# A cross-attention and low-rank FFN kernel: written-out engine orders for the first three batches, up and down weights in eight pieces, and a value chunk ahead of the row transposes

## The chip, the cores and the metric

The kernel runs on one core of a Trainium2 chip. The metric is the device time of one execution in microseconds, from that core. The kernel before took 1092.97 us in the median of three runs (1090.92 to 1093.71). Engines: PE is TensorE, ACT is ScalarE, DVE is VectorE, POOL is GpSimd, SP is SyncE, which only issues DMAs here. `PEld` is TensorE's weight load.

## The reference

Thirty-two independent batches, each a 128 x 1024 matrix in float32 (channels by time), pass through a windowed cross-attention and a routed low-rank FFN:

```python
x = x + xattn(layernorm(x), ctx, Wq, bq, Wk, bk, Wv, bv, Wo, bo)
x = x + ffn(layernorm(x), gate_w, lora_A, lora_B)

# xattn: q = Wq x + bq, k = Wk ctx + bk, v = Wv ctx + bv (128 x 128 weights)
k_win, v_win = k[:, :, idx], v[:, :, idx]       # window of 16 keys per query, zero padded
dots = einsum('bhdt,bhdtw->bhtw', q, k_win) * scale     # 8 heads of 16
out  = einsum('bhtw,bhdtw->bhdt', softmax(dots), v_win)
return Wo out + bo

# ffn: rows of 1024, 8 experts of rank 64, top 2 of them
w_full = top-2 of softmax(x @ gate_w.T), normalised
out = sum_e w_full[:, e] * (x @ lora_A[e].T @ lora_B[e].T)
```

The layer norms run along the 1024 columns.

## The kernel before

**Tiles.** A batch is one tile of 128 partitions by 1024 columns. Every matmul operand of the projections and of the FFN is split into two float32r parts, hi and lo (`x_split`, `ctx_split`, `attn_split`, `mid_split`, `ht_split`, and for the weights `w_split`, `down_split`, `up_split`), and a product is three passes (hi hi, hi lo, lo hi). ScalarE writes the hi part (a copy that rounds), and VectorE or GpSimd the lo part (exact minus hi). The weights are split once, at the start, in pieces: each lands in a buffer that is not needed yet, is split from there, and the buffer is then free for its own use. Before, there are six pieces: `w_split` (512 columns), two of `up_split` (2048 each) and three of `down_split` (2048, 1024, 1088).

**Attention.** The queries are laid out as small diagonal blocks (`q_diag`), two batches deep. The scores of a batch come in four chunks of 512 columns on PSUM banks `bank_b0` and `bank_b1` in turn, each opened with the mask in it: `scores_chunk(b, m)`, 64 small float32 matmuls, 128 in the trace. VectorE takes the maximum and subtracts it (`scores_shift`), ScalarE does the exponentials in `prob`, VectorE sums and inverts (`weights_sum`), GpSimd scales (`weights_norm`), VectorE transposes into `prob_t` (`weights_transpose`). The value chunks, `weighted_chunk(b, m)`, go to `bank_b2` and `bank_b3`; ScalarE (`even_heads`) and VectorE (`join_heads`) bring each into `attn`. The values themselves are transposed by VectorE (`v_transpose`) and scattered by four DMAs into the block-diagonal `v_diag` (`place_v`).

**FFN.** The second norm's result `xn2` is transposed on PE (eight 128 x 128 blocks into `bank_a`, `L371`), split, multiplied by the down weights (`down(0, f)` holds the router's logits too), routed on VectorE (`choose_experts`, `gate_experts`; ScalarE's `gap_exponential` in between), weighed (`h_sb`), transposed, split and multiplied by the up weights (`up`). `add_mixture` adds to the residual, and SP stores it.

**Order of the work.** Each engine has a list written out by hand, and semaphores alone join the lists. A step works on five batches at once: in step n, `cur` is batch n (values, scores and the first two value chunks), `ahead` is n+1 (queries, keys, first scores), `later` is n+2 (loads and first norm), `prev` is n-1 (last value chunks, output projection, second norm) and `old` is n-2 (FFN). Steps -2 to 33 are the same code with parts left out where a batch does not exist. PE is unrolled fully; the other engines loop over steps 3 to 28, two per turn. Each engine runs its list strictly in order, so an instruction that waits holds all behind it. `bank_c` is shared by the four projections, which therefore wait for each other's evacuation: `place_q` (`L575`), `evacuate_k` (`L583`), `evacuate_v` (`L591`), `residual` (`L848`). In many places PE's wait for a chunk is written one matmul product early, so that it stands ahead of the last product before the chunk:

```python
for n in range(6):
    if n == 5 and cur:
        open_scores(cur, 3)
    last = project_pass(n, bank_c, 1, ctx_split)
```

## Time and profile before

| what | value |
|---|---|
| median of three runs | 1092.97 us |
| the profiled execution | 1090.87 us |
| its span in the trace | 1089.1 us |
| PE busy | 1003.8 us, 92% |
| VectorE busy | 842.4 us, 77% |
| ScalarE busy | 573.7 us, 53% |
| GpSimd busy | 429.5 us, 39% |
| mean granted clock of TensorE | 0.978 |

Busy time is that of instructions, without waits. The granted clock is a share of 2.4 GHz, and 0.5 is the lower level, 1.2 GHz. A row of the timeline gives the start, the time from the first start to the last end, engine, line, operation, tiles, shapes and count; in brackets stands the idle time of the engine just ahead of it, and what ended that ("issue" where the trace shows no releaser). float32 matmuls are two passes each in the trace, so a score chunk counts x128 and a value chunk x36.

### The profile page before, as it was taken

How to read it: one execution, taken by the hardware profiler on the slowest of the kernel's cores; microseconds unless marked ns; L12 is line 12 of the kernel's file. 1: busy time of each engine (PE TensorE's matmuls, PEld its weight loads, DVE VectorE, ACT ScalarE, POOL GpSimd, SP SyncE). 2: the span in 40 equal slices, each digit the busy share in tenths (PEclk: the TensorE clock that was granted, in tenths of full speed). 3: DMA queues.
4: the chain of work that ended last, by engine and by line, in shares of the span. 5: the costliest groups of instructions: out<-in, count | busy, mean ns of one | idle time of the engine just before them, and what ended most of it. 6: DMA issues, size and time to landing. Idle time of an engine off the chain costs nothing.

```text
span 1089.1 us, 54694 instructions
## 1 busy us (share of the span) xinstructions
PE 1003.8 (92%) x24452; PEld 867.9 (80%) x24452; DVE 842.4 (77%) x1890; ACT 573.7 (53%) x809; POOL 429.5 (39%) x370
## 2 busy tenths in 40 slices
PE   4657999999999999999999999999999999999977
PEld 2545888888888888888888888888888888888865
DVE  2545798888888888888878878887877888887853
ACT  4544565556655555565555546555555655555321
POOL 3375344344343443443434334343434434342210
PEclk9867999999999999999999999999999999999989
DMA  5321233333321333333223333322333332232210
GB/s 195 101 80 36 84 83 82 100 100 101 100 76 67 79 84 97 100 100 87 66 88 81 81 100 100 95 60 83 81 83 100 100 83 69 89 81 63 61 40 39
DMA packets 157289, 92.47 MB, mean 85 GB/s; under 512 B 139680, under 2 KB 139808, under 8 KB 156704
## 3 DMA queue, kind: packets, MB, share of 16 engines
q1 hardware_dynamic: 157088, 89.25, 28.7%
q8 instruction: 192, 3.15, 1.2%
q14 instruction: 9, 0.07, 0.0%
HBM read 55.16 MB, written 16.78 MB: 66 GB/s over the span
## 4 chain that ended last, share of the span: by engine, by line
PE 88%; issue 3%; POOL 3%; ACT 2%; DVE 2%; SPq 1%; DMA 1%; DVEq 0%
PE bank_a L312 35%; PE bank_b L362 18%; PE bank_c L312 17%; PE bank_b L341 14%; PE bank_a L371 4%; POOL x_split L974 1%; POOL down_split L940 1%; SPq L248 0%; POOL up_split L940 0%; DMA ident<-ident_in 0%; DMA v_diag<-v_t 0%; ACT up_split L542 0%; ACT raw L622 0%; ACT x_split L622 0%; DVE stats L715 0%
## 5 line engine op out<-in xcount | busy, mean ns | idle before, releaser
L362 PEld LDWEIGHTS bank_b<-prob_t,v_diag 64*64 64x64 f32 x4608 | 193.4, 136 | 48.0 <-issue 33.1
L362 PE MATMUL bank_b<-prob_t,v_diag 64*64 64x96 f32 (+2 forms) x4608 | 208.8, 242 | 20.7 <-DVE attn L732 9.0
L312 PE MATMUL bank_a<-down_split,mid_split 128*128 128x264 f32 (+1 forms) x1536 | 214.9, 289 | 1.1 <-issue 0.5
L947 POOL TENSOR_TENSOR prob<-prob,row_inv 128x512 f32<-128x512 f32 x128 | 134.6, 1052 | 186.7 <-DVE row_inv L802 185.6
L312 PEld LDWEIGHTS bank_a<-down_split,mid_split 128*128 128x128 f32 x1536 | 194.8, 189 | 8.2 <-issue 1.6
L341 PEld LDWEIGHTS bank_b<-k_sb,q_diag 32*32 32x32 f32 x16384 | 155.5, 105 | 57.2 <-issue 51.4
L341 PE MATMUL bank_b<-k_sb,q_diag 32*32 32x32 f32 x16384 | 172.3, 195 | 25.2 <-issue 22.7
L312 PE MATMUL bank_a<-up_split,ht_split 128*128 128x512 f32 x768 | 192.2, 400 | 3.0 <-DVE ht_split L837 3.0
L312 PEld LDWEIGHTS bank_a<-up_split,ht_split 128*128 128x128 f32 x768 | 139.4, 188 | 32.9 <-ACT ht_split L637 3.4
L953 POOL TENSOR_TENSOR ctx_split<-raw,ctx_split 128x1024 fp32r<-128x1024 f32 x31 | 73.3, 2366 | 183.9 <-ACT ctx_split L603 183.9
L809 DVE STREAM_TRANSPOSE prob_t<-prob 128x768 f32<-128x768 f32 x128 | 124.1, 969 | 23.8 <-POOL prob L947 23.7
L798 DVE TENSOR_REDUCE row_sum<-prob 128x16 f32<-128x512 f32 x128 | 85.3, 667 | 52.0 <-ACT prob L562 52.0
L575 ACT ACTIVATE q_diag<-bank_c,bq_scaled,consts 128x1024 f32<-128x1024 f32 x64 | 73.6, 1200 | 67.3 <-PE bank_c L312 67.3
L784 DVE TENSOR_REDUCE row_max<-bank_b 128x16 f32<-128x512 f32 x128 | 86.3, 674 | 26.6 <-PE bank_b L341 26.3
L312 PE MATMUL bank_c<-ctx_split,w_split 128*128 128x512 f32 x384 | 105.6, 412 | 0.7 <-DVE w_split L705 0.7
L583 ACT ACTIVATE k_sb<-bank_c,bias 128x1024 f32<-128x1024 f32 x32 | 35.6, 1114 | 130.3 <-PE bank_c L312 130.3
L968 POOL TENSOR_TENSOR attn_split<-attn,attn_split 128x1024 fp32r<-128x1024 f32 x32 | 75.6, 2362 | 69.4 <-ACT attn_split L610 69.4
L974 POOL TENSOR_TENSOR x_split<-raw,x_split 128x1024 fp32r<-128x1024 f32 x32 | 78.4, 2449 | 57.0 <-ACT raw L622 57.0
L562 ACT ACTIVATE prob<-prob 128x512 f32<-128x512 f32 x128 | 80.1, 626 | 35.2 <-DVE prob L790 32.8
L790 DVE TENSOR_TENSOR prob<-bank_b,row_max 128x512 f32<-128x512 f32 x128 | 88.5, 692 | 4.4
L312 PEld LDWEIGHTS bank_c<-ctx_split,w_split 128*128 128x128 f32 x384 | 73.1, 198 | 16.9 <-DVE w_split L705 2.3
L959 POOL TENSOR_TENSOR rstd<-var_eps,consts 128x1 f32<-128x1 f32 x64 | 35.2, 551 | 108.0 <-DVE var_eps L724 107.9
(74 smaller groups left out, 1265.6 us busy)
## 6 DMA issues: line engine op xcount, KB each, us to landing
v_diag<-v_t SPq DMA_DIRECT2D x128, 132.0 KB
raw<-x SPq DMA_DIRECT2D x32, 512.0 KB, 4.6
resid_pair<-x SPq DMA_DIRECT2D x32, 512.0 KB, 5.4
out<-resid_pair SPq DMA_DIRECT2D x32, 512.0 KB, 3.2
raw<-ctx SPq DMA_DIRECT2D x31, 512.0 KB, 3.3
...
```

Of the source, the lines that this page charges most:

```text
L312: return nc.tensor.matmul(dst, st[:, s, st_cols], mv[:, m, mv_cols], start=start and n == 0, stop=stop and n == 2)
L341: last = nc.tensor.matmul(bank_b[m % 2][rows, t * KT:(t + 1) * KT], q_diag[rows, cur.parity, n, :], keys[rows, n * QT:n * QT + KT], start= ...
L362: last = nc.tensor.matmul(bank_b[2 + m % 2][rows, lo * PW:hi * PW], value_blocks(b)[rows, n, :], prob_t[rows, at:at + (hi - lo) * KT], sta ...
L562: nc.scalar.activation(weights_of(m), weights_of(m), ACT.Exp).then_inc(exp_done, 1)
L575: nc.scalar.activation(q_diag[:, ahead.parity, :, h * QT:(h + 1) * QT], bank_c[:].rearrange("p (n i) -> p n i", i=QT), ACT.Identity, bias= ...
L784: nc.vector.tensor_reduce(row_max[:, cols], scores, AX_X, ALU.max).then_inc(max_done, 1)
L790: nc.vector.tensor_tensor(weights_of(m), scores, row_max[:, cols].unsqueeze(2).broadcast_to([P, CT, KT]), ALU.subtract).then_inc(shifted, 1)
L798: nc.vector.tensor_reduce(row_sum[:, cols], weights_of(m), AX_X, ALU.add).then_inc(sum_done, 1)
L809: nc.vector.transpose(prob_t[:, m * PC:(m + 1) * PC], prob[:, m % 2 * PC:(m % 2 + 1) * PC]).then_inc(prob_t_done, 1)
L947: nc.gpsimd.tensor_tensor(weights_of(m), weights_of(m), row_inv[:, cols].unsqueeze(2).broadcast_to([P, CT, KT]), ALU.mult).then_inc(prob_d ...
L968: nc.gpsimd.tensor_tensor(attn_split[:, 1, :], attn[:], attn_split[:, 0, :].bitcast(F32), ALU.subtract).then_inc(attn_lo, 1)
L974: nc.gpsimd.tensor_tensor(x_split[:, 1, :], raw[:], x_split[:, 0, :].bitcast(F32), ALU.subtract).then_inc(xn_lo, 1)
```

## The change

Three things are changed.

1. The steps -2 to 1 are gone. In their place every engine has a function `head(b0, b1, b2, b3)`, a list of its own for the first batches, which ends where step 2 begins. In it K and V of batch 0 go to `bank_a`, `bank_c` being used by its queries.
2. The up and down weights come in eight pieces of 1024 to 1056 columns, all issued before any other batch's data. They land in `q_diag`'s second half, `prob_t`, the two residual buffers and a new buffer `stage`. VectorE splits `w_split` only; the other eight lo parts are GpSimd's. `v_diag` is cleared whole at the start; context of batch 1 goes to `xn2` and not to `raw`.
3. In the steps the order changes on every engine. On PE `weighted_chunk(prev, 2)` comes ahead of the eight transposes of `xn2` and no longer behind them, and the waits for a chunk stand right at it. On ScalarE `attention_hi`, `write_mask(cur, 1)` and `gap_exponential` come ahead of `place_q`, and `even_heads(cur, 1)` moves into the next step. On VectorE, `weights_transpose(cur, 1)` goes behind `weigh_experts` and `second_norm` ahead of `weights_transpose(cur, 2)`. On GpSimd `attention_lo` comes ahead of `weights_norm(cur, 1)`.

On GpSimd, from the norm of batch 2 to the second norm of batch 0, before (`xn2` and `spare` are buffers of weight pieces):

```order
L959 TENSOR_TENSOR rstd<-var_eps,consts 128x1
L962 TENSOR_TENSOR shift<-var_eps,rstd 128x1
L947 TENSOR_TENSOR prob<-prob,row_inv 128x16x32
L940 TENSOR_TENSOR down_split<-xn2,down_split 128x1024
L974 TENSOR_TENSOR x_split<-raw,x_split 128x1024
L940 TENSOR_TENSOR down_split<-spare,down_split 128x1088
L959 TENSOR_TENSOR rstd<-var_eps,consts 128x1
```

and after, the same engine's last rows up to that norm:

```order
L1093 TENSOR_TENSOR ctx_split<-raw,ctx_split 128x1024
L1110 TENSOR_TENSOR attn_split<-attn,attn_split 128x1024
L1080 TENSOR_TENSOR down_split<-stage,down_split 128x1056 x2
L1101 TENSOR_TENSOR rstd<-var_eps,consts 128x1
L1104 TENSOR_TENSOR shift<-var_eps,rstd 128x1
L1101 TENSOR_TENSOR rstd<-var_eps,consts 128x1
```

The last row of each is batch 0's second norm. `x_split` of batch 3 has gone from ahead of it to behind it.

On PE, the start of an even step, before (`bank_c<-ctx_split` is the value projection, the 64x rows are `weighted_chunk(prev, 2)`):

```order
L312 MATMUL bank_c<-ctx_split,w_split 128x512 x6
L371 MATMUL bank_a<-ident,xn2 128x128 x8
L362 MATMUL bank_b2<-prob_t,v_diag 64x64 x2
L362 MATMUL bank_b2<-prob_t,v_diag 64x96 x14
L362 MATMUL bank_b2<-prob_t,v_diag 64x32 x2
L341 MATMUL bank_b1<-k_sb0,q_diag 32x32 x64
```

and after:

```order
L351 MATMUL bank_c<-ctx_split,w_split 128x512 x6
L401 MATMUL bank_b2<-prob_t,v_diag 64x64 x2
L401 MATMUL bank_b2<-prob_t,v_diag 64x96 x14
L401 MATMUL bank_b2<-prob_t,v_diag 64x32 x2
L410 MATMUL bank_a<-ident,xn2 128x128 x8
L380 MATMUL bank_b1<-k_sb0,q_diag 32x32 x64
```

Only the value chunk and the transposes changed places.

On ScalarE, the middle of a step, before (`mid_split` is `rows_hi`, `gate` the router's exponential):

```order
L575 ACTIVATE q_diag<-bank_c,bq_scaled,consts 128x64x16 x2
L562 ACTIVATE prob<-prob 128x16x32
L567 ACTIVATE bank_b1<-mask 128x512
L556 ACTIVATE attn<-bank_b3,consts 128x256
L615 ACTIVATE gate<-top 128x1
L610 ACTIVATE attn_split<-attn 128x1024
```

and after:

```order
L620 ACTIVATE prob<-prob 128x16x32
L614 ACTIVATE attn<-bank_b3,consts 128x256
L672 ACTIVATE attn_split<-attn 128x1024
L625 ACTIVATE bank_b1<-mask 128x512
L677 ACTIVATE gate<-top 128x1
L635 ACTIVATE q_diag<-bank_c,bq_scaled,consts 128x64x16 x2
```

The attention's hi part went ahead of the router's exponential, and the queries' evacuation behind it.

The diff, cut to its core:

```diff
-        pieces = (piece(wqkvo, attn, w_split, 0, 4 * P),
-                  piece(up_w, prob_t[:, T:3 * T], up_split, 0, 2 * T),
-                  piece(up_w, resid_pair, up_split, 2 * T, 4 * T),
-                  piece(down_w, v_diag[:, BLOCKS * HALF_P:], down_split, 0, 2 * T),
-                  piece(down_w, xn2, down_split, 2 * T, 3 * T),
-                  piece(down_w, spare, down_split, 3 * T, FK * DW))
+        pieces = (piece(wqkvo, attn, w_split, 0, 4 * P),
+                  piece(up_w, q_spare, up_split, 0, T),
+                  piece(up_w, q_spare[:, T:], up_split, T, 2 * T),
+                  piece(up_w, prob_t[:, T:], up_split, 2 * T, 3 * T),
+                  piece(up_w, prob_t[:, 2 * T:], up_split, 3 * T, 4 * T),
+                  piece(down_w, resid[0], down_split, 0, T),
+                  piece(down_w, resid[1], down_split, T, 2 * T),
+                  piece(down_w, stage, down_split, 2 * T, 2 * T + LAST),
+                  piece(down_w, stage[:, LAST:], down_split, 2 * T + LAST, FK * DW))
...
 sync (SP)
+            def head(b0, b1, b2, b3):
+                load_x(b0); load_ctx(b0)
+                consts, load_piece(0), load_piece(1), bias, ident, mask
+                load_piece(2) ... load_piece(7)
+                load_ctx(b1); load_piece(8)
+                load_x(b1); place_v(b0); load_x(b2); load_resid(b0)
+                load_ctx(b2); place_v(b1); load_x(b3); load_ctx(b3)
             def step(later, ahead, cur, prev, old):
-                place_v(cur); raw <- x(later); resid <- x(prev); raw <- ctx(later); store(old)
+                place_v(cur); load_resid(prev); load_x(later); load_ctx(later); store(old)
...
 tensor (PE)
+            def head(b0, b1, b2, b3):
+                first_masks(); project_k(b0); project_q(b0); project_v(b0)
+                scores_chunk(b0, 0), (b0, 1), (b0, 2)
+                project_q(b1); scores_chunk(b0, 3); weighted_chunk(b0, 0)
+                project_k(b1); weighted_chunk(b0, 1)
+                scores_chunk(b1, 0), (b1, 1); project_v(b1)
+                weighted_chunk(b0, 2); scores_chunk(b1, 2); weighted_chunk(b0, 3)
+                project_q(b2); scores_chunk(b1, 3); project_k(b2)
+                weighted_chunk(b1, 0); scores_chunk(b2, 0)
+                project_o(b0); weighted_chunk(b1, 1)
             def step(later, ahead, cur, prev, old):
+                if cur:
+                    project_v(cur, (x1_done, old.count(2, 2)))
                 if prev:
                     open_weighted(prev, 2)
+                    weighted_chunk(prev, 2)
+                pe.wait_ge(xn2_done, old.count(1, 1))
...
+                transposes(bank_a, xn2, range(4, FK)).then_inc(xt_done, 1)
                 if cur:
                     open_scores(cur, 1)
...
 gpsimd (POOL)
+            nc.gpsimd.memset(v_diag[:], 0.0).then_inc(v_diag_zero, 1)
+            def head(b0, b1, b2, b3):
+                rows_norm(0, ..., b0); context_lo(b0); normal_lo(b0)
+                split_lo(1); split_lo(2); rows_norm(0, ..., b1)
+                split_lo(3); normal_lo(b1)
+                weights_norm(b0, 0); weights_norm(b0, 1); context_lo(b1)
+                split_lo(4); weights_norm(b0, 2); rows_norm(0, ..., b2)
+                split_lo(5); weights_norm(b0, 3); weights_norm(b1, 0)
+                normal_lo(b2); split_lo(6); weights_norm(b1, 1); weights_norm(b1, 2)
+                context_lo(b2); attention_lo(b0); split_lo(7); split_lo(8)
+                rows_norm(0, ..., b3); rows_norm(1, ..., b0); normal_lo(b3)
             def step(later, ahead, cur, prev, old):
-                norm(prev,3), context_lo, norm(cur,0), norm(cur,1), attention_lo, rows_norm(later), ...
+                norm(prev,3), norm(cur,0), context_lo, attention_lo, norm(cur,1), rows_norm(later), ...
...
 scalar (ACT), in step
+                if cur:
+                    exponentials(cur, 1)
+                if prev:
+                    even_heads(prev, 3)
+                    attention_hi(prev)
+                if cur:
+                    write_mask(cur, 1)
+                if old:
+                    gap_exponential(old)
                 if ahead:
                     place_q(ahead)
-                if cur:
-                    exponentials(cur, 1)
-                    write_mask(cur, 1)
-                if prev:
-                    even_heads(prev, 3)
-                if old:
-                    gap_exponential(old)
-                if prev:
-                    attention_hi(prev)
...
 vector (DVE), in step
-                    weights_transpose(cur, 1)
+                    weights_sum(cur, 2)
                 if old:
                     weigh_experts(old, 0)
                     weigh_experts(old, 1)
                 if cur:
-                    weights_sum(cur, 2)
+                    weights_transpose(cur, 1)
                     scores_shift(cur, 3)
...
```

In the heads several calls are drawn together on a line here, and ScalarE's and VectorE's heads, which follow the same batches, are left out.

## Rows read from the trace of the kernel before

**Rows 1.** The page's first table: busy us, share of the span, instructions of PE.

```profile
PE 1003.8 (92%) x24452; PEld 867.9 (80%) x24452; DVE 842.4 (77%) x1890; ACT 573.7 (53%) x809; POOL 429.5 (39%) x370
```

**Rows 2.** Busy time by stretch: length, then each engine's busy us, PE's clock, DMA share, GB/s.

```profile
0.00:101.50 101.50, 55.53 (x1432) 43.02 (x1432) 43.82 (x83) 46.74 (x55) 51.43 (x44) 0.82 0.33 107
...
134.60:1040.50 905.90, 882.31 (x22011) 767.82 (x22010) 754.34 (x1696) 501.16 (x716) 362.17 (x312) 1.00 0.31 85
...
1040.50:1089.10 48.60, 33.54 (x247) 28.68 (x245) 18.19 (x53) 7.20 (x12) 3.08 (x3) 0.92 0.12 44
```

**Rows 3.** Timeline of PE in the first 110 us.

```profile
12.04 2.93 PE L312 MATMUL bank_c<-ctx_split,w_split 128*128 128x512 f32 x6 [0.72 <-DVE w_split L705]
...
24.89 1.93 PE L341 MATMUL bank_b<-k_sb,q_diag 32*32 32x32 f32 x128 [2.48 <-ACT q_diag L575]
...
73.04 2.88 PE L362 MATMUL bank_b<-prob_t,v_diag 64*64 64x64 f32 x36 [8.66 <-DVE attn L732]
...
101.57 1.97 PE L371 MATMUL bank_a<-ident,xn 128*128 128x128 f32 x8 [7.94 <-ACT xn L631]
...
107.14 1.65 PE L312 MATMUL bank_c<-x_split,w_split 128*128 128x512 f32 x6
```

**Rows 4.** Timeline of ScalarE: the normalisation of x1 of batch 0.

```profile
100.28 1.24 ACT L631 ACTIVATE xn<-resid_pair,shift,rstd 128x1024 f32<-128x1024 f32 x1 [6.99 <-POOL shift L962]
```

**Rows 5.** GpSimd's groups in the first 101.5 us: count, busy us, mean ns, idle before.

```profile
L974 POOL TENSOR_TENSOR x_split<-raw,x_split 128x1024 fp32r<-128x1024 f32 x4 | 10.9, 2716 | 6.0 <-ACT raw L622 6.0
...
L947 POOL TENSOR_TENSOR prob<-prob,row_inv 128x512 f32<-128x512 f32 x8 | 8.4, 1048 | 6.9 <-DVE row_inv L802 6.9
...
L953 POOL TENSOR_TENSOR ctx_split<-raw,ctx_split 128x1024 fp32r<-128x1024 f32 x2 | 4.7, 2354 | 4.4 <-ACT ctx_split L603 4.4
...
L940 POOL TENSOR_TENSOR up_split<-resid_pair,up_split 128x2048 fp32r<-128x2048 f32 x1 | 4.6, 4557 | 5.5 <-ACT up_split L542 5.5
...
L959 POOL TENSOR_TENSOR rstd<-var_eps,consts 128x1 f32<-128x1 f32 x5 | 2.8, 553 | 10.7 <-DVE var_eps L724 10.7
```

**Rows 6.** The page's DMA issues: x; and GB/s in 40 slices of 412 to 419 us.

```profile
raw<-x SPq DMA_DIRECT2D x32, 512.0 KB, 4.6
...
GB/s 0 0 0 0 0 0 0 211 421 421 421 374 445 468 234 0 94 0 0 0 0 0 0 0 0 0 0 48 200 109 143 173 155 188 134 157 127 162 198 214
```

**Rows 7.** Timeline of step 12: VectorE's score shift and h_sb, PE's K and transposes.

```profile
425.59 0.69 DVE L790 TENSOR_TENSOR prob<-bank_b,row_max 128x512 f32<-128x512 f32 x1
...
431.35 0.72 DVE L773 TENSOR_TENSOR h_sb<-bank_a,pick 128x256 f32<-128x256 f32 x2
...
429.39 1.55 PE L312 MATMUL bank_c<-ctx_split,w_split 128*128 128x512 f32 x6
...
432.12 0.66 PE L371 MATMUL bank_a<-ident,h_sb 128*128 128x128 f32 x4
```

**Rows 8.** Timeline of PE: waits named issue in steps 9, 10, 12 and 31.

```profile
322.94 1.64 PE L312 MATMUL bank_c<-x_split,w_split 128*128 128x512 f32 x6 [1.15 <-issue]
...
354.44 0.25 PE L341 MATMUL bank_b<-k_sb,q_diag 32*32 32x32 f32 x3 [1.10 <-issue]
...
417.10 0.26 PE L341 MATMUL bank_b<-k_sb,q_diag 32*32 32x32 f32 x8 [0.63 <-issue]
...
1018.51 0.67 PE L341 MATMUL bank_b<-k_sb,q_diag 32*32 32x32 f32 x55 [0.53 <-issue]
```

**Rows 9.** DMA queues: instruction packets on the page, and from 414.7 to 416.0 us.

```profile
q8 instruction: 192, 3.15, 1.2%
...
q8 instruction: 1, 0.02, 4.5%
```

**Rows 10.** Timeline of the step without a current batch: PE's o, ScalarE's fourth even_heads and gate.

```profile
1053.43 2.90 PE L312 MATMUL bank_c<-attn_split,w_split 128*128 128x512 f32 x6 [4.68 <-issue]
...
1045.69 0.47 ACT L556 ACTIVATE attn<-bank_b,consts 128x256 f32<-128x256 f32 x1 [1.48 <-PE bank_b L362]
...
1049.67 0.30 ACT L615 ACTIVATE gate<-top 128x1 f32<-128x1 f32 x1 [3.51 <-DVE top_atf L746]
```

601 lines of the change are left out of this document (362 added, 239 removed).

## The prediction

> **What bounds the kernel now.** The page's first table comes first: TensorE (PE) has 1003.8 us of the 1089.1 us span [rows 1], so a gain is either PE idle time or PE running at its lower clock. The table by stretch says where these are [rows 2]. From 134.6 to 1040.5 us PE works 882.3 of 905.9 us at full clock. In the first 101.5 us it works 55.5 at a mean granted clock of 0.82, so 46 us are idle; in the last 48.6 us it works 33.5. The timeline of PE shows what the head's waits are [rows 3]: 8.66 us before batch 0's third value chunk, 7.94 us before the first transposes of x1 (batch 0). I call "the mark" the start of the query projection of batch 3, at 107.14; from there the steps run evenly, so the head's gain is how much earlier the mark comes.
>
> What ended the 7.94 us is ScalarE's normalisation of x1 at 100.28 [rows 4], which waited for GpSimd's list: x_split of batch 3 and the last piece of down_split stand ahead of batch 0's second norm there.
>
> **Head, floor.** GpSimd's new list up to batch 0's second norm holds, at the durations of [rows 5]: 7 weights_norm of 1.05 (7.3), 3 context_lo of 2.35 (7.0), 3 normal_lo of 2.35 (7.0; the row's mean of 2.7 holds one of 3.8 that met a VectorE pass), attention_lo 2.35, eight pieces of 1024 to 1056 columns, 4.56/2 = 2.28 per 1024 (18.4), and 5 pairs rstd and shift of 0.8 (4.1): 46.2 us. Batch 0's statistics are there at about 7 (x lands 4.6 us after its issue at 0.74 [rows 6], then 1.6 of statistics). So normalise_x1 can't come before 53.3, against 100.28: the gain is at most 47.
>
> **Head, ceiling.** If PE stayed at its lower clock all through, its list up to the mark takes 10 projections of 2.93, 9 score chunks of 1.93, 7 value chunks of 2.88 [rows 3], 66.8 us, after the mask matmuls (some 3.8, done at 12.6 since mask lands at about 8.8), then transposes and a score chunk, 3.9: the mark at 83.3, 24 us earlier. Lost waits could add to that, 3 or 4 us.
>
> **Head, walked through.** Each step is the later of its inputs and its place on its engine, with the durations above, 1.13 to 1.24 per ScalarE pass of 1024 columns [rows 4] and 1.35 for a scores_shift, its two instructions as one [rows 7].
> - Weights: 6.4 MB in pieces go out at once; at the 421 GB/s that a busy stretch shows [rows 6] they have landed at about 19.5. x of batch 1 is issued at 12.9 (after batch 0's x_lo) but stands behind them and lands at about 21. VectorE has its statistics ahead of batch 0's v_transpose, and GpSimd its rstd ahead of the third piece: both idle to 21, GpSimd from 17.6. This wait is new and costs some 4 us of GpSimd.
> - Batch 1 normalised 25.7; batch 0's first exponentials and masks 26 to 28; x_lo of batch 1 28.0; weights_norm of chunks 0 and 1 30.1; first value chunk 31 to 33; k of batch 1 evacuated 35.5 to 38.5 (the spread is PE's clock, since PE stood from 23 to 27).
> - VectorE is then the narrow one: from scores_shift(b1, 0) at 38 to 40 to the fourth join_heads of batch 0 it has 11 to 12 us without a gap. So attn of batch 0 is whole at 50 to 53, context_lo(b2) ends at 53 to 55, attention_lo(b0) 55 to 58, the last two pieces 60 to 63.
> - PE: k of batch 2 needs that context_lo, after some 4 us of waiting, so at the lower clock: then value chunk, scores, o of batch 0 to 62 to 65; residual, statistics, rstd to 66 to 69; normalise_x1 at 66 to 69; the value projection and chunk of batches 2 and 1 fit beside it; v evacuated at 70 to 73.
> The mark comes at 70 to 73, with nothing allowed for waits on instructions, of which the head before has four (1.6 to 2.5 us). I take 75: 32 earlier. In the step itself context of batch 3 is issued only when x_lo of batch 3 is done (71), lands some 4 us on, and ScalarE's rows_hi(old, 1) stands behind it: 1 us back. **Head: -31, between -20 and -43.**
>
> **The evenly running steps.** PE's list holds the same matmuls. The value chunk (1.5 us) and the eight transposes (1.0) change places, so scores chunk 1 starts at the same distance from the value projection. The waits that stood one pass early now stand right at a chunk. On ScalarE place_q moves behind gap_exponential, to about 424.8 to 427.1 in the step of 412.8; its reader, the key projection, comes at 429.4 [rows 7]: 2.3 us of cover. weights_transpose(cur, 1) moves behind weigh_experts and ends at about 433.0, its reader at 434.1. rows_lo(1) ends near 420, its reader at 421.9. attention_lo comes ahead of weights_norm(cur, 1), so earlier. The tightest place stays: h_sb is done at 432.07, PE's transposes start at 432.12 [rows 7]; the row ahead of it is a weights_sum (0.92) in place of a transpose (0.97). Term: 0, if all cover holds; one place that lost 0.3 us in each of 30 steps would cost 9.
>
> **Instruction waits.** Nearly all 23.6 us that PE idles there [rows 2] are waits of 0.3 to 1.3 us that the profile calls "issue", one per step, from 322.94 on in or at the end of scores chunk 1 [rows 8]. The number of matmuls left after the wait grows by 2.5 a step: 3 at 354.44, 8 at 417.10, 55 at 1018.51. That is a boundary in the instruction stream: 192 packets of instructions for 2 x 24452 PE instructions [rows 1, 9] is one per 255, and the built step is 1541 instructions, 5 (2.5 matmuls with their loads) over 6 x 256. One such packet lies at 414.7 to 416.0, ahead of the wait that ended at 417.10 [rows 8, 9]. In the changed program a step is 1540 instructions: the drift is 4, and counted from the same start the boundary meets the chunk's end in step 11 and not 9. That is 21 waits of about 1.0 and not 23: -2. If the start lies otherwise, all 30 steps could wait, +7; or the slower transposes ahead of the chunk cover the fetch, down to -20. Term: -2.
>
> The Trainium skill, "Runtime: NRT & Kernel Launch", section "Instruction fetch mechanics", says that instructions come in blocks of 256 while the present ones run, and that crossing a boundary costs something "mostly hidden". By that this term would be 0 and the time 1057. The trace agrees on the block, not on the hiding.
>
> **Tail.** In the step without a current batch PE waits 4.68 us for o of batch 31 [rows 10]: ScalarE had the fourth even_heads at 1045.69, then gap_exponential, which waited 3.51 us for the router, until 1049.67, and attention_hi behind it. Now attention_hi comes first: join_heads after even_heads ends at 1046.7, so it starts at 1046.8 and not 1049.88, 3.0 earlier. The earlier value chunk may give up to 1 more, and o ran 2.90 us at the lower clock where 1.6 is the full rate, up to 1.3. Term: -4, between -2 and -6.
>
> **Sum.** The profiled execution took 1090.87 us, 1.8 around its span: 1090.87 - 31 + 0 - 2 - 4 = 1053.9. It lies 2.1 below the median of the runs, 1092.97; from that the same sum gives 1056. I predict 1055.
>
> **Rivals.**
> - *A cold head.* PE never gets long enough work to leave the lower clock and also waits: for it, the mean granted clock of the head before was 0.82 [rows 2]; against it, the new lists put two or three batches' chunks next to each other. The mark at 85 to 90, total 1065 to 1070. The Trainium skill, "TensorE: Matmul & The Clock Gate", Part 1, has the throttled clock as the default and activity as what lifts it; the trace agrees, PE's first matmuls run at half rate [rows 3].
> - *Waits for instructions grow.* The boundary falls into a score chunk in all steps, or the weight traffic holds fetches back in the head: 7 to 10 us, total 1062 to 1065.
> - *Slower than before: place_q behind the router.* ScalarE is in order: join_heads(prev, 3), attention_hi, write_mask, gap_exponential, place_q, exponentials(cur, 2), evacuate_k. If that chain is late, so is the key projection and after it everything on PE, in each of 29 steps. It must be late by its cover of 2.3 and 1.3 us more (37 us over 29 steps) to eat the gain; the page has ScalarE at 53% busy, which speaks against it. With 5 us late per step the time is about 1055 + 29 x 2.7 = 1133.
> - *The head isn't shorter*, since x of batch 1 behind the weights and GpSimd's larger share (18.4 us of pieces against some 14) eat what the order gives: total about 1088, counted as no change.
>
> **How the numbers follow.** Forecast 0.74 (own range 1044 to 1064), cold head 0.10, instruction waits 0.09, place_q 0.04, no shorter head 0.03. Range 1042 to 1069: it takes in the forecast's terms at their ends and most of the two rivals next to it. A difference of 0.3%, 3.3 us, is what a measurement here can tell. Faster 0.93, same 0.03, slower 0.04.
>
> **What would show it.** Right: the mark near 75; ScalarE's xn2 near 68 to 71; GpSimd idle near 18 to 22 for batch 1's statistics; PE busy about 97% between and its "issue" waits beginning about step 11, growing by 2 matmuls a step; PE's wait for o in the tail below 2 us. Wrong: a releaser other than "issue" on PE in the even steps, a step longer than 31.3, or a mark past 85.

## The result, and the profile of the changed kernel

The changed kernel takes 1065.7 us (median, 1061.5 to 1066.8) against 1093.0, a ratio of 0.9751 (95% interval 0.9734 to 0.9768): 27 us faster, 10.7 more than the 1055 forecast. It is inside the range given, and just outside the forecast's own range of 1044 to 1064. The profiled execution took 1065.6, its span is 1063.8. Of all executions in this document one, of e12_x_early, took 1193.6 us at a mean granted clock of 0.749 and is in no number below.

Busy time by stretch of the changed kernel, cut at the query projection of batch 3 ("the mark") and at that of batch 31. The columns are those of [rows 2].

```profile
0.00:73.60 73.60, 50.26 (x1605) 40.07 (x1605) 43.05 (x85) 49.63 (x62) 54.83 (x48) 0.88 0.44 142
73.60:963.90 890.30, 863.60 (x21392) 744.41 (x21392) 766.43 (x1655) 503.08 (x704) 359.16 (x310) 1.00 0.30 87
963.90:1063.80 99.90, 87.84 (x1469) 75.51 (x1457) 64.06 (x150) 29.80 (x47) 18.27 (x17) 0.94 0.17 49
```

The books, from the starts of these projections: the mark comes 33.5 us earlier (73.60 against 107.14 in [rows 3]); the 28 steps between take 890.4 us instead of 880.9 (107.14 to 987.99 before), so 9.5 are lost; what follows takes 99.8 instead of 101.1, 1.3 gained. 33.5 - 9.5 + 1.3 is the 25.3 us between the spans. The head did more than was said and the even steps, which were to cost nothing, took back more than a quarter of it. The 33.5 are of one execution: seven of the kernels below (changed, e2, e4, e5, e6, e9, e10) have the same head on all engines, and their marks lie between 73.4 and 78.5, a gain of 29 to 34 us (the last 6 us ahead of the mark belong to step 2, whose orders differ).

The head, in the timelines of PE, VectorE, GpSimd and ScalarE, to be set against [rows 3] and [rows 4]:

```profile
20.90 1.29 DVE L811 BATCH_NORM_STATS2 stats<-raw 128x6 f32<-128x512 f32 x2 [10.83 <-DMA raw<-x]
...
22.76 0.55 POOL L1101 TENSOR_TENSOR rstd<-var_eps,consts 128x1 f32<-128x1 f32 x1 [5.78 <-DVE var_eps L820]
...
57.46 2.90 PE L351 MATMUL bank_c<-ctx_split,w_split 128*128 128x512 f32 x6 [4.30 <-POOL ctx_split L1093]
...
69.81 1.24 ACT L691 ACTIVATE xn<-resid_pair,shift,rstd 128x1024 f32<-128x1024 f32 x1 [0.76 <-POOL shift L1104]
...
71.11 1.09 PE L410 MATMUL bank_a<-ident,xn 128*128 128x128 f32 x8 [0.70 <-ACT xn L691]
...
73.60 1.64 PE L351 MATMUL bank_c<-x_split,w_split 128*128 128x512 f32 x6 [0.18 <-ACT v_sb L652]
```

The two long waits of [rows 3] are gone. x of batch 1 does stand behind the weights until 20.9, GpSimd idles 5.8 us for it, and PE waits 4.3 us for the context of batch 2, as walked.

An even step, over all four engines, with what PE waited for. This answers to [rows 7] and [rows 8]:

```profile
427.95 2.38 POOL L1110 TENSOR_TENSOR attn_split<-attn,attn_split 128x1024 fp32r<-128x1024 f32 x1 [5.17 <-ACT attn_split L672]
428.13 2.23 DVE L844 CAST top_atf<-top_at 128x2 f32<-128x2 uint32 x1
...
430.39 0.29 ACT L677 ACTIVATE gate<-top 128x1 f32<-128x1 f32 x1 [2.03 <-DVE top_atf L844]
430.59 2.28 ACT L635 ACTIVATE q_diag<-bank_c,bq_scaled,consts 128x1024 f32<-128x1024 f32 x2
...
433.19 1.53 PE L351 MATMUL bank_c<-ctx_split,w_split 128*128 128x512 f32 x6
...
437.01 0.31 PE L380 MATMUL bank_b<-k_sb,q_diag 32*32 32x32 f32 x11 [1.17 <-issue]
...
453.34 0.26 PE L380 MATMUL bank_b<-k_sb,q_diag 32*32 32x32 f32 x6 [0.23 <-issue]
```

The reader is to see three things. VectorE's cast of 2 columns takes 2.23 us while GpSimd runs attention_lo. The gate exponential on ScalarE waits for that cast, place_q for the exponential, and q is placed at 432.87, 0.32 us ahead of the key projection, where I had counted 2.3 us of cover. And PE's waits named issue now come at two places in a step: in score chunk 1 as before (453.34, 6 matmuls before its end), but also in score chunk 3 (437.01, 11 before its end), where the kernel before has none in any of these steps. Summed over the 28 steps, chunk 1 and what follows it directly wait 7.6 us (20.7 before), chunk 3 and what follows it 14.4 us in 20 steps.

### The profile page after: what moved, and what is told of

Same layout as the page of the kernel before. It is cut to its first block, busy times and chain, and to the rows that moved or that the text cites. A ratio compares the mean times of both kernels' runs of the same rounds, so it can differ in the third digit from the quotient of the medians.

```text
span 1063.8 us, 54664 instructions
## 1 busy us (share of the span) xinstructions
PE 1001.7 (94%) x24452; PEld 860.0 (81%) x24452; DVE 873.5 (82%) x1889; ACT 582.5 (55%) x812; POOL 432.3 (41%) x373
## 4 chain that ended last, share of the span: by engine, by line
PE 85%; issue 6%; DVE 5%; ACT 2%; DMA 1%; POOL 1%; DVEq 0%; SPq 0%
PE bank_a L351 34%; PE bank_b L401 17%; PE bank_c L351 16%; PE bank_b L380 13%; PE bank_a L410 5%; DVE stats L811 1%; DMA raw<-x 1%; DVE h_sb L871 0%; DVE row_max L882 0%; DMA prob_t<-ctx 0%; DVE row_sum L896 0%; DVE pick L857 0%; ACT v_sb L652 0%; DVE resid_pair L950 0%; POOL x_split L1116 0%
## 5 line engine op out<-in xcount | busy, mean ns | idle before, releaser
L401 PEld LDWEIGHTS bank_b<-prob_t,v_diag 64*64 64x64 f32 x4608 | 189.5, 134 | 34.9 <-issue 26.4
L401 PE MATMUL bank_b<-prob_t,v_diag 64*64 64x96 f32 (+2 forms) x4608 | 204.7, 239 | 1.0 <-issue 0.9
L351 PE MATMUL bank_a<-up_split,ht_split 128*128 128x512 f32 x768 | 195.8, 405 | 3.0 <-DVE ht_split L937 3.0
L351 PEld LDWEIGHTS bank_a<-up_split,ht_split 128*128 128x128 f32 x768 | 142.2, 192 | 33.9 <-ACT ht_split L697 3.6
L1110 POOL TENSOR_TENSOR attn_split<-attn,attn_split 128x1024 fp32r<-128x1024 f32 x32 | 76.1, 2380 | 151.5 <-ACT attn_split L672 151.5
L1116 POOL TENSOR_TENSOR x_split<-raw,x_split 128x1024 fp32r<-128x1024 f32 x32 | 76.9, 2405 | 99.3 <-ACT raw L684 99.3
L614 ACT ACTIVATE attn<-bank_b,consts 128x256 f32<-128x256 f32 x128 | 59.5, 465 | 89.9 <-PE bank_b L401 89.9
L351 PE MATMUL bank_c<-ctx_split,w_split 128*128 128x512 f32 x372 | 99.0, 402 | 4.3 <-POOL ctx_split L1093 4.3
L830 DVE SCALAR_TENSOR_TENSOR attn<-bank_b,consts,attn 128x256 f32<-128x256 f32 x128 | 58.4, 458 | 34.0 <-ACT attn L614 34.0
L351 PEld LDWEIGHTS bank_c<-ctx_split,w_split 128*128 128x128 f32 x372 | 69.0, 192 | 17.9 <-issue 4.4
```

The lines of the kernel that those rows point to most:

```text
L351: return nc.tensor.matmul(dst, st[:, s, st_cols], mv[:, m, mv_cols], start=start and n == 0, stop=stop and n == 2)
L401: last = nc.tensor.matmul(bank_b[2 + m % 2][rows, lo * PW:hi * PW], value_blocks(b)[rows, n, :], prob_t[rows, at:at + (hi - lo) * KT], sta ...
L1110: nc.gpsimd.tensor_tensor(attn_split[:, 1, :], attn[:], attn_split[:, 0, :].bitcast(F32), ALU.subtract).then_inc(attn_lo, 1)
L1116: nc.gpsimd.tensor_tensor(x_split[:, 1, :], raw[:], x_split[:, 0, :].bitcast(F32), ALU.subtract).then_inc(xn_lo, 1)
```

## The experiments

Medians in us, ratio to the kernel before with its 95% interval (the kernel before was measured again beside each group of runs, 1091.2 to 1093.4), the start of batch 3's query projection, the 28 steps from there to batch 31's, and PE's waits above 0.1 us in them, summed from the timelines: for instructions ("issue") and for h_sb. "Rest" is from batch 31's projection to the end of the span. From the mark on, the columns are of the one profiled execution.

| kernel | time | ratio | mark | 28 steps | issue | h_sb | rest |
|---|---|---|---|---|---|---|---|
| before | 1093.0 | 1 | 107.1 | 880.9 | 23.4 | 0 | 101.1 |
| changed | 1065.7 | 0.975 (0.973-0.977) | 73.6 | 890.4 | 23.7 | 2.8 | 99.8 |
| e1_all_old | 1063.0 | 0.973 (0.969-0.977) | 77.8 | 881.7 | 23.3 | 0 | 103.1 |
| e2_pe_old | 1078.6 | 0.987 (0.983-0.991) | 78.5 | 898.2 | 33.9 | 4.2 | 101.2 |
| e3_others_old | 1057.1 | 0.968 (0.964-0.971) | 75.1 | 877.3 | 9.2 | 0 | 104.6 |
| e4_transposes_first | 1079.4 | 0.988 (0.985-0.992) | 78.2 | 898.0 | 34.2 | 3.3 | 101.1 |
| e5_q_placed_early | 1056.0 | 0.966 (0.963-0.968) | 75.5 | 880.5 | 9.8 | 9.0 | 97.7 |
| e6_gap_first | 1068.3 | 0.977 (0.975-0.980) | 75.4 | 891.2 | 10.7 | 16.7 | 100.5 |
| e7_1536 | 1041.6 | 0.954 (0.951-0.956) | 72.0 | 862.8 | 0 | 0 | 103.1 |
| e8_1536_shifted | 1052.9 | 0.962 (0.959-0.965) | 76.1 | 871.3 | 4.8 | 0 | 104.0 |
| e9_combined | 1030.8 | 0.943 (0.940-0.946) | 74.1 | 857.0 | 0 | 0 | 98.0 |
| e10_combined_transposes_first | 1026.6 | 0.940 (0.937-0.943) | 73.4 | 850.4 | 0 | 0 | 97.4 |
| e11_before_1536 | 1062.3 | 0.972 (0.968-0.975) | 106.8 | 851.3 | 0 | 0 | 103.3 |
| e12_x_early | 1025.4 | 0.940 (0.938-0.942) | 76.2 | 849.4 | 0 | 0 | 99.3 |

My theory after the result was that the 9.5 us lie in the new orders of the steps: some in transitions between kinds of matmul around the moved value chunk, some in VectorE's cast and q placed late. The rival was that a shorter head by itself makes the steps longer. The first four runs split the orders by engine.

**All step orders as before, new head** (e1_all_old).

```diff
-                if prev:
-                    open_weighted(prev, 2)
-                    weighted_chunk(prev, 2)
                 pe.wait_ge(xn2_done, old.count(1, 1))
...
                     even_heads(cur, 0)
+                    even_heads(cur, 1)
```

> The new beginning (orders of the first three batches, weights in eight pieces), followed by the earlier kernel's step orders on all five engines. Theory A (the 9.5 us lost over the 28 even steps come from the new step orders): the steps take 31.46 us again instead of 31.80, the query projection of batch 3 stays at 73.6, the time is 1055 to 1058. Rival B (the loss comes along with the shorter beginning, through the clock or the place of the instruction blocks, whatever the step orders): the steps stay at 31.8 and the time at 1064 to 1067.

The steps take 881.7, within 1 us of the kernel before: the orders are the cause, the head is not. The time was 5 us above what I expected: the mark comes at 77.8 and the rest of the run is 3 us longer. Of the 4.2 us by which the mark is late, 2.3 are there already at the key projection of batch 2 (59.80 against 57.46), ahead of every step, so the old orders account for the other 1.9 at most. So the new beginning alone is worth 29 us, as much as the whole change. Which of its parts (the order, the eight pieces, the buffers) gives how much was not tested.

**TensorE's order as before, the others new** (e2_pe_old).

```diff
+                        if n == 5 and cur:
+                            open_scores(cur, 3)
                         last = project_pass(n, bank_c, 1, ctx_split)
```

(with the transposes first, as in the next but one)

> The changed kernel with TensorE's steps in the earlier order: row transposes ahead of the value chunk, and the four hoisted waits back inside the passes; the other engines keep the new orders. Theory A1 (0.15 us per step are lost to two dearer transitions between kinds of matmul around the moved value chunk): 4 us back, 1061 to 1062, with VectorE's cast of 2.2 us and the 0.4 us waits for h_sb still there. Theory A2 (the waits that are no longer hoisted also stop the sequencer ahead of score chunk 3, so that the next instruction block is asked for late): the waits for instructions at chunk 3 go as well, 1054 to 1058. Rival (neither matters): 1064 to 1067.

1078.6: both theories fail, in sign. PE's old order is 13 us slower beside the other engines' new ones, 7.8 of them in the 28 steps.

**TensorE's order new, the others as before** (e3_others_old).

```diff
-                    attention_hi(prev)
...
                     gap_exponential(old)
-                if ahead:
-                    place_q(ahead)
+                if prev:
+                    attention_hi(prev)
```

> The changed kernel with ScalarE, VectorE, GpSimd and SyncE in the earlier step orders, TensorE alone in the new one. Theory C (GpSimd's lower half of the attention output now runs beside VectorE's routing chain, whose cast goes from 0.17 to 2.23 us, and place_q ends 2 us later): the cast is 0.2 us again, TensorE waits nowhere for h_sb, 3 us back from that and 2 to 4 from instruction blocks asked for earlier at score chunk 3: 1058 to 1062. Rival (these cover only each other and TensorE's own order is the whole loss): 1064 to 1066.

1057.1, with 28 steps of 877.3: less than either kernel's, although the first of them takes 37.7 us, with 4.0 of waiting for `mid_split` in it. The cast takes 0.17 us again and PE nowhere waits for h_sb. The waits for instructions fell from 23.7 to 9.2, more than I had expected.

**Only the value chunk back behind the transposes** (e4_transposes_first).

```diff
-                if prev:
-                    open_weighted(prev, 2)
-                    weighted_chunk(prev, 2)
                 pe.wait_ge(xn2_done, old.count(1, 1))
...
                 transposes(bank_a, xn2, range(4, FK)).then_inc(xt_done, 1)
+                if prev:
+                    open_weighted(prev, 2)
+                    weighted_chunk(prev, 2)
```

> The changed kernel with one edit: value chunk 2 of the previous batch behind the eight row transposes again; no wait is hoisted. Theory A1 (transitions between kinds of matmul): from V's first matmul to score chunk 1's first it takes 3.87 us instead of 4.02, 28 to 30 times, 4 us in all: 1061 to 1062. Rival (the transposes were waiting for xn2 and now wait again, or nothing changes): 1065 or more.

1079.4, the same as with all of TensorE's old order: the hoisted waits do nothing. The theory's small number is right all the same, since in the steps in which nothing waits for instructions this kernel needs 30.8 us and the changed one 31.0 to 31.1. But the waits for instructions rise from 23.7 to 34.2: 20.3 at chunk 1 instead of 7.6, and 13.0 instead of 14.4 at chunk 3. With the value chunk ahead, the boundary in chunk 1 costs less. The timelines give a reason, which is an estimate: the 8 transposes are 16 instructions in 1.09 us, 68 ns each, the value chunk 72 in 1.58 us, 22 each, the score chunk 256 in 1.29 us, 5 each. A block of 256 that ends 20 matmuls before the end of score chunk 1 takes 2.0 us with value matmuls ahead of the scores and 2.7 us with the transposes there. A block that takes longer gives the next one more time to arrive.

The four runs make a table of two by two over the 28 steps: others old, PE old 881.7 and new 877.3; others new, PE old 898.2 and new 890.4. PE's new order gained 4 to 8 us there; the other engines' orders lost 13 to 17. The first of the 28 steps blurs this (32.3, 37.7, 30.7 and 32.2 us). Over the other 27 the table reads 849.4 and 839.7, then 867.5 and 858.2: PE's order gains 9.3 to 9.7 and the other engines' orders lose 18.2 to 18.5, whatever the other half is.

**q placed early** (e5_q_placed_early). The next runs look for the cause in the other engines' orders, and at the boundaries themselves.

```diff
                 if cur:
                     exponentials(cur, 1)
+                if ahead:
+                    place_q(ahead)
                 if prev:
                     even_heads(prev, 3)
                     attention_hi(prev)
...
-                if ahead:
-                    place_q(ahead)
```

> The changed kernel with one edit on ScalarE: place_q stands right behind the exponentials of chunk 1, ahead of even_heads 3 and attention_hi, so that q is placed some 5 us before the key projection instead of 0.3 us. Theory D (TensorE's sequencer stands at the wait for q_out, and asks for the next block of instructions only once it is past it): the waits for instructions in score chunk 3 (about 10 us over the 28 even steps, 15 of them) go or fall under 3 us in all, those in chunk 1 stay; the 28 steps take 879 to 883 us instead of 890.4, the time is 1055 to 1059. Theory C alone (only VectorE's late h_sb counts): waits for h_sb shrink or grow by 1 to 2 us, 1063 to 1067, and chunk 3's waits for instructions are there as before.

1056.0, 28 steps of 880.5, and at score chunk 3 no step waits for instructions any more. The instruction packet shows why. In the changed kernel, queues from 432.7 to 434.5 us, and from 434.5 to 436.0:

```profile
DMA packets 0, 0.00 MB, mean 0 GB/s; under 512 B 0, under 2 KB 0, under 8 KB 0
...
q8 instruction: 1, 0.02, 3.8%
```

The packet begins at 434.6, 1.4 us after the key projection (433.19). With q placed early it begins at 431.7, 0.6 us ahead of that projection:

```profile
432.32 1.53 PE L351 MATMUL bank_c<-ctx_split,w_split 128*128 128x512 f32 x6
433.78 1.29 PE L380 MATMUL bank_b<-k_sb,q_diag 32*32 32x32 f32 x128
435.50 0.66 PE L410 MATMUL bank_a<-ident,h_sb 128*128 128x128 f32 x4 [0.42 <-DVE h_sb L871]
```

and its queues from 431.6 to 433.2 us:

```profile
q8 instruction: 1, 0.02, 5.4%
```

PE's program is the same in both; only ScalarE's order differs. So a wait that costs PE nothing (q was ready 0.3 us before it was needed) delays the request for instructions. That the sequencer stands at it and can't run ahead is my reading; the timeline has no row of the sequencer there. What took the place of these waits is h_sb, 0.37 us late in 24 steps, which they had hidden.

**The gate's exponential ahead of attention_hi** (e6_gap_first).

```diff
                     even_heads(prev, 3)
-                    attention_hi(prev)
                 if cur:
                     write_mask(cur, 1)
                 if old:
                     gap_exponential(old)
+                if prev:
+                    attention_hi(prev)
```

> The changed kernel with one edit on ScalarE: the gap exponential ahead of attention_hi, as in the earlier kernel; place_q stays behind both. Theory C (GpSimd's lower half of the attention output meets VectorE's cast): the cast takes 0.2 us again, h_sb is 1 us or more earlier, TensorE's 2.8 us of waits for h_sb (7 steps, and hidden in others) are gone; place_q ends about as late as now, so by theory D the waits in score chunk 3 stay: 1061 to 1064. Rival (the clash moves with the instruction to another of VectorE's, as pick took 1.6 us in the earlier kernel): h_sb is no earlier, 1064 to 1067.

1068.3: what theory C expected fails, and its rival is right, since the clash moved to another victim. What the cast alone does to h_sb is not shown by this. Timeline of this kernel:

```profile
431.05 0.17 DVE L845 CAST top_atf<-top_at 128x2 f32<-128x2 uint32 x1
...
432.57 2.37 POOL L1111 TENSOR_TENSOR attn_split<-attn,attn_split 128x1024 fp32r<-128x1024 f32 x1 [6.86 <-ACT attn_split L672]
...
433.55 2.43 DVE L858 TENSOR_SCALAR pick<-consts,top_atf,gate 128x8 f32<-128x8 f32 x2
```

The cast is short, but attention_lo now meets pick, whose two instructions take 2.43 us, where they took 0.48 in the changed kernel's step at 432.21. They end at 435.98, 0.03 us after the weights_norm that GpSimd runs right behind attention_lo (434.90, 1.05 long), and h_sb is 0.4 us later still: 16.7 us of waits in 26 steps. I was also wrong on q: its placing moved up by 1.1 us, which left 1.4 us ahead of the key projection, and that was enough for the waits in chunk 3 to go.

**A step of 1536 instructions** (e7_1536). Made from the kernel with the others' old orders.

```diff
-                pe.wait_ge(xt_hi, old.count(2, 1))
                 pe.wait_ge(xt_lo, old.count(2, 1))
...
-                pe.wait_ge(xt_hi, old.count(2, 2))
                 pe.wait_ge(xt_lo, old.count(2, 2))
...
-                pe.wait_ge(ht_hi, old.count(1, 1))
                 pe.wait_ge(ht_lo, old.count(1, 1))
...
-                    open_scores(ahead, 0)
+                    pe.wait_ge(mask_set, ahead.count(CHUNKS, -1))
```

> The kernel with TensorE's new order and the other engines' earlier step orders (1057.1 us), with four waits that others imply taken out of each of TensorE's steps, so that a step has 1536 instructions, six blocks of 256, instead of 1540: the block boundaries stay 24 instructions into score chunk 1 and 36 into chunk 3 in every step. Theory E (the waits for instructions come where a boundary has drifted near the end of a score chunk): no such wait in any even step, steps of 30.6 to 30.7 us throughout, 9 us of waits and some stretching gone, 1042 to 1048. Rival (the waits depend on something else, such as the DMA traffic or the length of the run): 1055 to 1059, with waits of 0.4 to 1.0 us in the later steps.

1041.6. There isn't one wait for instructions in the even steps, which behind the first (36.0, with 3.6 of waiting for `mid_split`) alternate between about 30.53 and 30.69 us to the end. Four waits taken out, at which PE nowhere waits behind the first step, are worth 15.5 us, 14.5 of them in the 28 steps. It is not the waits' own time: where no instruction wait disturbs it, a step of e3_others_old takes the same 30.55 to 30.70.

**The same, with the boundary elsewhere** (e8_1536_shifted).

```diff
+                for n in range(168):
+                    pe.wait_ge(pads_zero, 1 + n % 7)
                 pe.wait_ge(pads_zero, 7)
```

(two waits make one instruction)

> The kernel of 1536 instructions per step, with 84 more wait instructions at the very start of TensorE's program, where it waits for the first loads anyway: each block boundary moves 84 instructions earlier against the work, to 60 instructions before the end of score chunk 1 (and 48 before that of chunk 3). Theory E: a wait of 0.8 to 1.0 us in score chunk 1 in every one of the even steps (as in steps 20 to 22 of the kernel it comes from, with the boundary at that place), 22 to 28 us in all: 1065 to 1073. Rival (the place of the boundary does not matter): the same time as the unshifted kernel within 2 us.

1052.9: the place of the boundary decides, by 8.5 us over the 28 steps, but a third of what I had said. The waits in score chunk 1 always come 24 matmuls before its end, in nine steps only, 0.2 to 0.7 us each (four more, of 0.2 to 0.3, lie in a value chunk):

```profile
204.06 0.39 PE L383 MATMUL bank_b<-k_sb,q_diag 32*32 32x32 f32 x24 [0.23 <-issue]
235.30 0.39 PE L383 MATMUL bank_b<-k_sb,q_diag 32*32 32x32 f32 x24 [0.51 <-issue]
327.74 0.39 PE L383 MATMUL bank_b<-k_sb,q_diag 32*32 32x32 f32 x24 [0.18 <-issue]
359.00 0.39 PE L383 MATMUL bank_b<-k_sb,q_diag 32*32 32x32 f32 x24 [0.51 <-issue]
```

In e3_others_old, from which both are made, the step with 22 matmuls left waits 1.0 us and the next, with 24 left, 0.2. I had taken the 0.9 of the neighbours; no other place was tried.

**Both fixes in the changed kernel** (e9_combined), and VectorE's order at h_sb:

```diff
+                if old:
+                    weigh_experts(old, 0)
+                    weigh_experts(old, 1)
                 if cur:
                     weights_sum(cur, 2)
-                if old:
-                    weigh_experts(old, 0)
-                    weigh_experts(old, 1)
```

> The changed kernel (its orders on all engines) with three edits: q placed early on ScalarE, VectorE's weigh_experts ahead of weights_sum of chunk 2 (h_sb 0.9 us earlier), and the four implied waits taken out of TensorE's steps (1536 instructions). Theories D and E together: no waits for instructions and none for h_sb in the even steps, which take 30.6 us each; with the query projection of batch 3 at 75.5, the first step 31.8 and the tail as in the run with q placed early, the time is 1031 to 1036. Rival (the cast that takes 2.2 us moves with what follows it, and h_sb stays 0.37 us late in each step): 1040 to 1044.

1030.8: no wait of either kind, although the cast still takes its 2.2 us. Of its three edits only q placed early was run alone on the changed kernel.

**The same with the transposes first** (e10), the edit of the fourth run.

> The combined kernel with one edit more: value chunk 2 behind the row transposes again. By the theory that the moved value chunk costs 0.15 to 0.2 us per step in transitions, and that it paid in the changed kernel only because it slowed the blocks of 256 instructions that end in score chunk 1, it is now a loss: 5 us faster than the combined kernel, 1026 to 1031, steps of 30.4 us. Rival (moving the value chunk ahead hides something else, since undoing it cost 14 us in the changed kernel): slower than the combined kernel by 5 us or more.

1026.6, 28 steps of 850.4, all but three of them 30.36. The edit that cost the changed kernel 13.7 us (7.6 in the 28 steps) gains 4 here (6.6 in the 28 steps, of which 1.0 is a wait for `mid_split` in e9's first one; over the other 27 it is 5.1, 0.19 a step). Of these 0.19, 0.15 lie between the value projection's first matmul and score chunk 1's, 4.02 us in e9 and 3.87 in e10. The row of the stretch (columns as in [rows 2]) has PE busy in 850.35 of 850.35 us, at full clock:

```profile
73.36:923.71 850.35, 850.35 (x21400) 742.84 (x21392) 760.40 (x1654) 498.87 (x701) 359.53 (x308) 1.00 0.32 90
```

**The kernel before with steps of 1536** (e11_before_1536). Five waits out; open_scores(cur, 1) stands behind the transposes.

```diff
-                    pe.wait_ge(xt_hi, old.count(2, 1))
...
-                    pe.wait_ge(xt_hi, old.count(2, 2))
...
-                    pe.wait_ge(ht_hi, old.count(1, 1))
...
-                            open_scores(ahead, 0)
+                            pe.wait_ge(mask_set, ahead.count(CHUNKS, -1))
...
-                pe.wait_ge(v_placed, b.count(16 * PAIRS, 16 * PAIRS))
+                if m != 2:
+                    pe.wait_ge(v_placed, b.count(16 * PAIRS, 16 * PAIRS))
```

> The earlier kernel, in its orders, with five waits that others imply taken out of each of TensorE's steps (open_scores of chunk 1 stands behind the transposes for that): 1536 instructions per step in place of 1541, boundaries 24 instructions into score chunk 1 and 36 into chunk 3. Theory E: all of the 23 us of waits for instructions in the even steps go, the 28 steps take 852 us instead of 881: 1063 to 1067, as fast as the changed kernel. Rival (the waits are partly cover for other things that then wait): 1072 to 1082.

1062.3, faster than the changed kernel without any of its new orders:

```profile
106.82:958.07 851.25, 851.25 (x21399) 742.82 (x21393) 731.59 (x1652) 492.49 (x700) 357.90 (x309) 1.00 0.32 90
```

The 28 steps fall by 29.6 us, 6 more than the waits that the timeline lists: the matmuls around a late block are also spread out (PE busy 857.3 before, 851.3 now). That it could be the five waits themselves and not the boundary is ruled out by the undisturbed steps: 30.39 to 30.40 us in the kernel before, 30.39 to 30.40 here.

**x of batch 1 ahead of the late weights** (e12_x_early), in the fastest kernel:

```diff
+                load_ctx(b1)
+                load_x(b1)
                 load_piece(5)
                 load_piece(6)
                 load_piece(7)
-                load_ctx(b1)
                 load_piece(8)
-                load_x(b1)
...
-                split_hi(5)
                 place_q(b0)
                 evacuate_v(b0)
                 normalise_x(b1)
+                split_hi(5)
```

> The combined kernel with the transposes first (1026.6 us) and one edit in its beginning: SyncE issues the context and x of batch 1 ahead of weight pieces 5 to 8, and ScalarE rounds piece 5 behind normalise_x of batch 1. Theory F (x of batch 1 lands at 21.2 us only because it queues behind the late pieces, and GpSimd's idle 6 us until 23.1 are that): x lands near 17 us, rstd of batch 1 comes at 19 to 20 instead of 23.1, and the query projection of batch 3 starts 2 to 4 us earlier than 73.4: 1022 to 1025. Rival (GpSimd and ScalarE have the late pieces to work off anyway, which now come later, and catch up nowhere): batch 3's query projection within 1 us of 73.4 or later, 1026 to 1029.

1025.4, between the two expectations, and inside the spread of e10's own executions (1022.95 to 1027.55). The first half of the theory came true:

```profile
15.86 1.29 DVE L808 BATCH_NORM_STATS2 stats<-raw 128x6 f32<-128x512 f32 x2 [5.83 <-DMA raw<-x]
...
17.72 0.55 POOL L1098 TENSOR_TENSOR rstd<-var_eps,consts 128x1 f32<-128x1 f32 x1 [0.77 <-DVE var_eps L817]
...
49.39 0.69 DVE L879 TENSOR_REDUCE row_max<-bank_b 128x16 f32<-128x512 f32 x1 [2.36 <-PE bank_b L380]
52.93 2.06 POOL L1084 TENSOR_TENSOR prob<-prob,row_inv 128x512 f32<-128x512 f32 x2 [3.58 <-DVE row_inv L897]
...
70.82 1.36 PE L410 MATMUL bank_a<-ident,xn 128*128 128x128 f32 x8 [2.13 <-ACT xn L688]
```

rstd comes 5.4 us earlier (17.7 against 23.1), but the mark 2.8 us later (76.2 against 73.4). GpSimd does not keep its lead: at 52.93 it waits 3.58 us for VectorE, which waited 2.36 us for PE's scores at 49.39. So what GpSimd gains at the start it loses to waiting for the other two.

The 2.8 us can't be put down to the edit. In the seven kernels with one and the same head the key projection of batch 2 starts anywhere from 55.99 (e10) to 60.50 us (e5), here at 58.27. e10 is the earliest of them, and it differs in when PE ran at the lower clock: in the window from 42.3 to 45.6 us the granted clock is 1.00 in e10, 0.50 in the changed kernel and 0.79 here. The same window in e10, then in this kernel:

```profile
42.30:45.60 3.30, 3.18 (x54) 2.59 (x56) 2.98 (x6) 1.89 (x3) 2.87 (x3) 1.00 0.15 57
```

```profile
42.30:45.60 3.30, 2.44 (x21) 1.54 (x21) 2.98 (x6) 2.34 (x3) 2.87 (x3) 0.79 0.33 124
```

A gain or a loss of 1 or 2 us in the head is below what one trace of each can tell.

## Why the prediction was right, and where it was not

**Head, -31 between -20 and -43: right in size and steps.** Measured -33.5, normalise_x1 at 69.8 (said 66 to 69), the new wait for x of batch 1 as said, PE waiting some 4 us for the context of batch 2 as said. The walk gave 70 to 73 and the trace 73.6; the 2 to 5 us that I added for instruction waits were too many (two of 2.1 us are there, at 24.0 and 42.6). Some of the closeness is luck: with the same head other kernels have the mark at up to 78.5. That the wait for x cost "some 4 us of GpSimd" is true of the engine; in the last run, without it, the time did not fall beyond the spread. The walk's "6.4 MB" of weights are weights (4.5 MB) and the first batches' x and context together.

**Even steps, 0: this is the step that failed.** I had written "2.3 us of cover" for place_q, having placed the gap exponential from the router's chain as it ran before. But attention_hi moved ahead of that chain, so attention_lo starts 1.7 us earlier in the step (427.95, 6.8 us after the query projection; in the kernel before 425.85, 8.5 us after it), and meets the cast: 0.17 became 2.23 us. The cover shrank to 0.3 us and h_sb came 0.4 us late. Placing q early alone took the 28 steps from 890.4 to 880.5 (e5), as much as they had lost. I did price exactly such a place ("one place that lost 0.3 us in each of 30 steps would cost 9") and gave it no weight. In the kernel before, the sign of this clash was there to be read: its two pick instructions take 0.80 us each, in the changed one 0.29 (groups of the kernel before, then of the changed one, where the cast has taken over):

```profile
L759 DVE TENSOR_SCALAR pick<-consts,top_atf,gate 128x8 f32<-128x8 f32 x64 | 48.5, 800 | 1.2
```

```profile
L857 DVE TENSOR_SCALAR pick<-consts,top_atf,gate 128x8 f32<-128x8 f32 x64 | 15.5, 289 | 1.2
...
L844 DVE CAST top_atf<-top_at 128x2 f32<-128x2 uint32 x32 | 67.9, 2120 | 1.1
```

The value chunk "at the same distance" was wrong too: ahead of the transposes it costs 0.19 us a step (e9 against e10), most of it in transitions between kinds of matmul, with no wait listed.

Two of the three signs that I had named for "wrong" came: a releaser other than "issue" on PE in the even steps (h_sb, in 7 of them), and steps longer than 31.3 us (31.8 in the mean). The time stayed in the range all the same, since the head's surplus of 2.5 us made up for a part, but it is 1.7 us outside the forecast's own range.

**Instruction waits, -2: right in total by luck.** The drift of 2 matmuls a step and the start at step 11 came out to the step: 357.29 in the changed kernel, then 2, 4, 6, 8 matmuls left. But there were 14 of them and not 21, of 0.2 to 1.0 us in place of 1.0. That goes with the value chunk's place (e4 has 20.3 us there), and fits the slower block with the transposes in it, which I had named, "down to -20". And new ones of 0.2 to 1.2 came in chunk 3, which I had not named:

```profile
277.52 0.18 PE L380 MATMUL bank_b<-k_sb,q_diag 32*32 32x32 f32 x1 [0.86 <-issue]
308.93 0.25 PE L380 MATMUL bank_b<-k_sb,q_diag 32*32 32x32 f32 x3 [0.77 <-issue]
...
357.29 1.67 PE L351 MATMUL bank_c<-x_split,w_split 128*128 128x512 f32 x6 [0.42 <-issue]
...
388.92 0.22 PE L380 MATMUL bank_b<-k_sb,q_diag 32*32 32x32 f32 x2 [0.19 <-issue]
```

13 us gained at the one place and 14 lost at the other left 23.7 against 23.4. The cause of the new ones, a late q, is the same step that failed above.

The books of the even steps, in the runs' numbers. Full work for PE is 850.4 us (e10). The changed kernel's 890.4 are that, 6.6 for the place of the value chunk (with the 1.0 of waiting in e9's first step), 9.9 that go with q placed early (e5), and 23.5 that go with steps of 1536 and weigh_experts first (e5 to e9), of which the timeline lists 9.0 as h_sb and 9.8 as issue. The kernel before has 29.6 over the 851.3 of its own work (e11), all from instruction blocks.

**Tail, -4 between -2 and -6: each part right, the sum given back.** PE waits 1.56 us for o where it waited 4.68, and o takes 1.61 where it took 2.90 [rows 10]; but the gain from the whole rest is 1.3. Windows of the two up products of the last batches, the third column being their length and the last but two the clock: the kernel before, then the changed one.

```profile
1063.20:1068.70 5.50, 5.50 (x24) 4.50 (x25) 0.69 (x1) 0.23 (x1) 0.00 (x0) 1.00 0.00 0
1079.60:1085.20 5.60, 5.60 (x24) 4.37 (x24) 0.69 (x1) 0.00 (x0) 0.00 (x0) 1.00 0.00 0
```

```profile
1034.10:1041.80 7.70, 7.70 (x24) 6.15 (x25) 0.69 (x1) 0.21 (x1) 0.00 (x0) 0.69 0.01 2
1052.70:1059.90 7.20, 7.19 (x24) 5.54 (x24) 0.69 (x1) 0.00 (x0) 0.00 (x0) 0.77 0.00 0
```

Both ran at 2.4 GHz throughout before; now the granted clock is 0.69 and 0.77 of it, which is 3.8 us back. The kernel before fell to the lower clock during its 4.7 us of waiting, and was back up for these. In the changed kernel the clock falls at 1032.1, after PE has waited 1.56 and 1.90 us at 1023.8 and 1029.8, ahead of the first of them, and comes back in the middle of it; it falls again at the start of the second. The kernel before, then the changed one:

```profile
1050.00:1053.40 3.40, 0.00 (x0) 0.00 (x0) 0.00 (x0) 0.91 (x1) 2.34 (x1) 0.61 0.00 0
1053.40:1056.30 2.90, 2.87 (x7) 2.32 (x8) 0.75 (x1) 0.00 (x0) 0.00 (x0) 0.50 0.02 6
```

```profile
1032.00:1034.10 2.10, 0.59 (x5) 0.23 (x3) 0.69 (x1) 1.51 (x2) 0.00 (x0) 0.52 0.00 0
1038.00:1041.80 3.80, 3.80 (x16) 3.08 (x15) 0.69 (x1) 0.00 (x0) 0.00 (x0) 0.88 0.02 4
1052.70:1055.00 2.30, 2.29 (x6) 1.82 (x7) 0.00 (x0) 0.00 (x0) 0.00 (x0) 0.50 0.00 0
```

In e5, with the same waits, the first of them took 7.10 us, the second ran at full clock again, 5.68, and the rest took 97.7; in e10 it took 97.4, 3.6 less than before. So the new orders can give 3 to 4 us here, and how much of it comes is a matter of where the clock falls. I had counted what the clock gives to o, and not what it then takes elsewhere.

**The rivals.** The cold head (1065 to 1070) gives the right time for the wrong reason: the mark was 11 us earlier than it needs. "Instruction waits grow" (1062 to 1065) is the nearest: the new place exists, though the sum did not grow. place_q behind the router was the right instruction with the wrong price: it never made the key projection late, it only took the sequencer's lead.
